# Layer-1 feed-forward on f16 halves, gate products joined to qkv, few-row products on 128 rows, unit addresses formed one triple ahead

## The chip, the core and the metric

The kernel runs on one core of a Trainium2 chip. The metric is the device time of one execution in microseconds (us). The core has five engines that run their own instruction queues in order and wait for each other on semaphores: TensorE (PE in the profile; PEld is its loading of the stationary operand), VectorE (DVE), ScalarE (ACT), GpSimd (POOL) and SyncE (SP).

## The reference, cut to what matters

The input is 32 sequences of 256 tokens, each token a vector of 128. Everything is a residual stream `x`, in f32:

```
x = x + 0.5 * L0_ffn(layernorm(x))      # 8 experts, top 2, and one shared
x = x + L0_attn(layernorm(x))           # linear attention, 32 heads, group norm
x = x + 0.5 * L0_ffn(layernorm(x))
x = x + 0.5 * L1_ffn(layernorm(x))      # 8 experts of 32 hidden values, top 1
x = x + L1_attn(layernorm(x))           # gated recurrence, 8 heads
x = x + 0.5 * L1_ffn(layernorm(x))

def L1_ffn(xt):
    top1 = argmax(xt @ Wg.T)
    xhat = layernorm(xt)
    for e in range(8):
        h = gelu((xhat * ln_scale[e] + ln_bias[e]) @ W1[e] + b1[e])
        y = y + (top1 == e) * (h @ W2[e] + b2[e])

# L1_attn: q, k, v = h @ Wq.T, h @ Wk.T, h @ Wv.T, and three gates
gate(W, b) = sigmoid(h @ W.T + b)        # W is 8 x 128, for beta, ig, og
```

## The kernel before

**Tiles and stages.** `x` stays on the chip. It is cut into 16 chunks of 512 tokens (T = 4 tiles of 128). Three stages overlap. The heads (three lanes) take a chunk through the norm, the gate, the shared expert and, between the two layer-0 feed-forwards, the attention. The units are the routed experts: tokens are scattered by expert to DRAM (`scatter`, an indirect DMA on POOL), fetched back in blocks of 128 and worked on in 76 units of four blocks; results are fetched with another indirect DMA (`fetches`). The last part of the span, from about 735 us, holds layer 1: the first feed-forward of a chunk (`ffn1` on the lanes mid), the attention's `front` and `back`, and the second feed-forward (`ffn1` on the lanes last). `ffn1` is called 32 times, `front` and `back` 16 times each.

**Order.** No engine chooses its order by itself. `turns` holds, for each engine, a string with one letter for each step (u and w are units, a to c heads, m n l o the feed-forwards of layer 1, t front, v back, r routing, s scatter, f fetch, p preparation, z a matmul whose result nobody reads). Each engine runs the steps in the order of its own string and waits, where it must, for a mark that another engine sets. PSUM has six banks that are handed out in turn; TensorE waits for the mark in `ring.free_at` before it writes a bank again.

**Layer-1 feed-forward on TensorE, `ffn1`.** Step 3 turns the normed chunk (4 transposes) and ACT copies it to `s.xt` in f32. Step 4 multiplies each tile by the gate, 4 f32 products of 8 columns (L740; the trace shows two records for each f32 product). DVE picks the best expert and builds a mask; step 6 turns it. Step 7 makes, for j = 0 and 1, one f32 product of 512 columns with the hidden weights of four experts (L757) and adds `sel1` times the mask (L759), which pushes all experts that were not chosen far below zero; the product with `sel1` contracts over 8 rows. ACT applies gelu. Step 8 multiplies by the second weights (L767, L771) and DVE adds the result to `x` (L1359).

**Layer-1 attention, `front`.** Step 0 turns the chunk. Step 1 first makes the gates, 4 f32 products of 24 columns into one bank (L791, read by DVE at L1387 to L1393), then q, k and v, 4 f32 products of 384 columns in a bank each (L797), which ACT copies out with the norm's factor (L1630, L1632). The gates' chain goes on from DVE's `zc` (L1393) to ACT's exponential (L1618).

**Biases.** Three outputs get a bias by a product that contracts over 3 rows, bf16 parts of the bias against ones: L544 (32 times), L613 (16) and L870 (16). An f32 product with full rows follows each.

**Units, `project`.** Each unit has two projections of two banks; for each bank and each of four blocks TensorE runs a triple: the high half of the weights against both halves of the rows, then the low half against the high half (L712). The place of the weights depends on the block's expert, held in a register; the two addresses of a triple, one in `w_hi` and one in `w_lo`, are computed by register instructions right in front of the matmul that uses them.

## Time and profile before

| | us |
|---|---|
| median of 3 runs | 1345.95 |
| lowest and highest run | 1339.19, 1349.72 |
| the profiled execution | 1347.7 |
| its span, first to last instruction | 1345.9 |

| engine | busy us | share of the span |
|---|---|---|
| PE | 1190.7 | 88% |
| DVE | 1059.0 | 79% |
| ACT | 807.7 | 60% |
| POOL | 676.6 | 50% |

The mean granted TensorE clock is 0.954 of full speed. Busy time is the union of an engine's records: matmuls are pipelined, so a matmul's own duration is longer than the distance from its start to the next one's. Where the cost of a matmul is wanted, the distance of the starts is read. The chain of waits is followed back from the last instruction, at each step to what released it.

### The profile page before, as it was taken

To read this page: it belongs to the slowest core of one execution; us is meant where nothing else is said; L and a number is where in the kernel's file an instruction comes from. 1 tells how busy PE (TensorE), PEld (TensorE's weight loads), DVE (VectorE), ACT (ScalarE), POOL (GpSimd) and SP (SyncE) were. 2 spreads that over 40 slices of the span, in tenths; PEclk is the share of its full clock that TensorE was granted. 3 is DMA by queue.
4 is the path that set the end of the run, shared out by engine and by line. 5 is a ranking of instruction groups with operands and counts; after the bars stand their busy time and mean duration, and the time that the engine had idled before them with its cause. 6 is when DMAs were issued, how large, how long until landed. Compare 5 with 4: busy or idle time off the path is not lost.

```text
span 1345.9 us, 39493 instructions
## 1 busy us (share of the span) xinstructions
PE 1190.7 (88%) x14344; PEld 918.0 (68%) x14344; DVE 1059.0 (79%) x3479; ACT 807.7 (60%) x1350; POOL 676.6 (50%) x727
## 2 busy tenths in 40 slices
PE   2866898898889979878998899999999999899997
PEld 1533776776677767656776678777777767676774
DVE  4888899988797989898878777767867689785652
ACT  1455677646645646555665777667746566556652
POOL 0157666777777777877777523415323634310100
PEclk9877999999999999999999999999979899899986
DMA  9001343533354332324343311222100111000001
GB/s 320 1 25 59 96 117 102 120 88 99 99 118 108 89 99 69 98 74 95 87 124 106 82 38 44 65 55 68 32 17 14 33 31 30 14 18 1 26 3 32
DMA packets 172958, 94.13 MB, mean 70 GB/s; under 512 B 98539, under 2 KB 163206, under 8 KB 172646
## 3 DMA queue, kind: packets, MB, share of 16 engines
q1 hardware_dynamic: 112838, 34.26, 10.5%
q0 software_dynamic: 16384, 33.59, 8.9%
q10 hardware_dynamic: 43552, 23.74, 6.4%
q8 instruction: 125, 2.05, 0.7%
q14 instruction: 59, 0.48, 0.1%
HBM read 25.98 MB, written 45.61 MB: 53 GB/s over the span
## 4 chain that ended last, share of the span: by engine, by line
PE 49%; DVE 30%; ACT 6%; issue 6%; POOL 5%; SPq 2%; DMA 2%; ACTq 0%; POOLq 0%; DVEq 0%
PE bank L712 10%; PE bank L757 4%; PE bank L771 3%; DVE heads_store L986 3%; DVE x L1018 2%; POOL rows L1725 2%; PE bank L728 2%; PE bank L928 2%; PE bank L797 2%; PE bank L740 2%; PE sums L945 2%; PE bank L559 2%; SPq L1791 1%; PE bank L759 1%; PE bank L841 1%
## 5 line engine op out<-in xcount | busy, mean ns | idle before, releaser
L1725 POOL DMA_INDIRECT rows<-store,r_slot x256 | 262.0, 1024 | 123.8 <-issue 73.3
L1742 POOL DMA_INDIRECT y_in<-ys,r_result x256 | 274.7, 1073 | 91.9 <-issue 71.2
L712 PE MATMUL bank<-u_xp,w_hi 128*128 128x128 f16 x2432 | 261.7, 222 | 10.7 <-DMA u_xp<-rows 3.8
L712 PE MATMUL bank<-u_xp,w_lo 128*128 128x128 f16 x1216 | 244.4, 221 | 0.0
L712 PEld LDWEIGHTS bank<-u_xp,w_hi 128*128 x2432 | 176.5, 99 | 35.2 <-issue 15.0
L712 PEld LDWEIGHTS bank<-u_xp,w_lo 128*128 x1216 | 120.0, 99 | 3.0
L1694 POOL TENSOR_SCALAR ve_last<-mv_last 128x4 f32<-128x4 f32 x16 | 3.3, 208 | 171.7 <-DVE mv_last L979 171.6
L559 PE MATMUL bank<-heads_store,w_hi 128*128 128x512 f16 x256 | 80.9, 399 | 5.7 <-DVE u_gated_odd L1330 3.1
L757 PE MATMUL bank<-heads_store,f_w1s 128*128 128x512 f32 x128 | 77.8, 692 | 0.7 <-ACT heads_store L1602 0.7
L1018 DVE SCALAR_TENSOR_TENSOR x<-y_in,r_weight,x 128x128 f32<-128x128 f32 x256 | 72.8, 346 | 1.6 <-DMA y_in<-ys,r_result 0.5
L771 PE MATMUL bank<-w_packed,heads_store 128*128 128x128 f32 x512 | 69.0, 291 | 0.0
L1495 ACT COPY heads_store<-bank 128x512 f32<-128x512 f32 x64 | 37.0, 584 | 52.3 <-PE bank L510 40.2
L771 PEld LDWEIGHTS bank<-w_packed,heads_store 128*128 128x128 f32 x512 | 64.6, 205 | 0.0
L1470 DVE TENSOR_TENSOR store<-store,bank 128x512 f32<-128x512 f32 x64 | 40.8, 680 | 25.9 <-ACT store L1671 15.9
L986 DVE TENSOR_SCALAR heads_store<-x,mv_head,rstd_head 128x128 f32<-128x128 f32 x192 | 55.3, 366 | 7.0 <-POOL rstd_head L1696 6.8
L1694 POOL TENSOR_SCALAR ve_front<-mv_front 128x4 f32<-128x4 f32 x16 | 3.2, 199 | 111.3 <-DVE mv_front L979 110.9
L1525 ACT ACTIVATE heads_store<-bank,sc 128x512 f32<-128x512 f32 x64 | 43.1, 681 | 21.3 <-PE bank L559 19.8
L1696 POOL TENSOR_TENSOR rstd_head<-ve_head,half_neg 128x4 f32<-128x4 f32 x48 | 53.3, 1111 | 4.0
L1606 ACT ACTIVATE heads_store<-bank,f_b1s 128x512 f32<-128x512 f32 x64 | 42.0, 686 | 20.3 <-PE bank L759 19.5
L559 PE MATMUL bank<-heads_store,w_lo 128*128 128x512 f16 x128 | 51.1, 399 | 0.0
L1498 ACT COPY heads_store<-bank 128x1024 f16<-128x1024 f16 x32 | 32.2, 1009 | 28.6 <-PE bank L518 27.8
L1064 DVE TENSOR_TENSOR heads_store<-bank,heads_store 128x512 f32<-128x512 f32 x64 | 43.1, 682 | 7.9 <-ACT heads_store L1525 7.4
(389 smaller groups left out, 3217.2 us busy)
## 6 DMA issues: line engine op xcount, KB each, us to landing
ys<-u_y_even ACTq DMA_DIRECT2D x38, 256.0 KB
ys<-u_y_odd ACTq DMA_DIRECT2D x38, 256.0 KB
u_xp<-rows SPq DMA_TRANSPOSE x304
x<-x_dram SPq DMA_DIRECT2D x16, 256.0 KB, 5.7
rows<-store,r_slot POOLq DMA_INDIRECT x256
y_in<-ys,r_result POOLq DMA_INDIRECT x256
out_dram<-x SPq DMA_DIRECT2D x16, 256.0 KB, 2.5
rows<-blank SPq DMA_DIRECT2D x48, 64.0 KB
```

The source lines that it names most:

```text
L559: ins = pe.matmul(B[:], wp[:, part, E, which, :], s.xp[:, xp, :], start=(n == 0), stop=(n == 2))
L712: ins = pe.matmul(B[:, of_block[j]], of_expert(wp, e, F16, part, which), xp_rows[:, xp, of_block[j]], start=(n == 0 and j == 0), stop=(n = ...
L757: pe.matmul(B[:], f1_w1s[:, j * P:(j + 1) * P], s.xt, start=True, stop=False, skip_group_check=True)
L771: ins = pe.matmul(Y[:, by_t[t]], s.gs[j][:, by_t[t]], const["f1_w2"][:, j, :], start=False, stop=(t == T - 1 and j == 1), skip_group_check ...
L986: ins = dve.tensor_scalar(out[:, t, :], xc(c)[:, t, :], s.mv[:, t, 0:1], s.rstd[:, t:t + 1], ALU.subtract, ALU.mult)
L1018: ins = dve.scalar_tensor_tensor(xt, y[:, t, i, :], w[:, i, t0 + t:t0 + t + 1], xt, ALU.mult, ALU.add)
L1064: s.by_vector.mark(dve.tensor_tensor(h, ring[s.name, "h", l, c, part, 1][:], h, ALU.mult), "h", l, c, part)
L1525: s.by_scalar.mark(act.activation(t, ring[s.name, "h", l, c, part, 0][:], ACT.Copy, scale=sc31[:]), "h", l, c, part)
L1606: mark(act.activation(s.gs[j], ring[s.name, "gelu", c, j][:], ACT.Gelu, bias=f1_b1s[:, j:j + 1]), "gelu", c, j)
L1696: s.by_pool.mark(pool.tensor_tensor(s.rstd[:], s.ve[:], half_neg[:], ALU.pow), "rstd", which, c)
L1725: pool.indirect_dma_start(row_dram[g], bass.IndirectOffsetOnAxis(route.slot[g][:, i, t:t + 1].bitcast(U32), 0), rows[:, groups[g].first * ...
L1742: pool.indirect_dma_start(fetch.y[i][:, t, k, :], None, y_dram[g], bass.IndirectOffsetOnAxis(route.result[g][:, k, t0 + t:t0 + t + 1].bitc ...
```

## The change

The layer-1 feed-forward keeps its turned input as two f16 halves in the same bytes: ACT copies the high half out of PSUM, and a new DVE step 3 subtracts it from the bank to give the low half. The gate and the hidden weights are scaled by powers of two, split into f16 halves in two new preparation steps, and each f32 product becomes three f16 products. The gelu gets a scale that undoes the factors. The bank of the transposes is free after DVE's subtraction.

The gates' 24 columns are put behind the 384 of q, k and v: one product of 408 columns for each tile. DVE reads the gates out of each tile's bank with one instruction for each tile instead of two for all, and ACT copies v after it.

`sel1`, `row_bias` and `ones_b` are used with all 128 rows, the unused rows of the first two being zero, so the mask and bias products contract over 128 rows.

`place_weights` lowers the two addresses of the next triple before the current triple's matmuls; the first triple's addresses are lowered with `load_experts`.

The indirect DMAs lose their bounds check. All the sequences in `turns` are new; the first steps of each stage stand at nearly the same place in them as before, and there are 12 letters z instead of 9.

```diff
-        f1_w1s = sb("f1_w1s", [P, E * 32])
+        f1_hi = sb("f1_hi", [P, E * 32], F16)
+        f1_lo = sb("f1_lo", [P, E * 32], F16)
+        g1_hi = sb("g1_hi", [P, E], F16)
+        g1_lo = sb("g1_lo", [P, E], F16)
...
+        a1_w = sb("a1_w", [P, 3 * D + 3 * NH1])
+        a1_wqkv, a1_wg = a1_w[:, 0:3 * D], a1_w[:, 3 * D:]
...
-        row_bias = sb("row_bias", [3, 3, D], BF16)
+        row_bias = sb("row_bias", [P, 3, D], BF16)
...
+            s.xp = s.xt.bitcast(F16).rearrange("p (k n) -> p k n", k=2)
...
-                    pe.matmul(Y[:], ones_b[0:3, :], row_bias[:, 0:1, :].broadcast_to([3, T, D]), start=True,
+                    pe.matmul(Y[:], ones_b[:], row_bias[:, 0:1, :].broadcast_to([P, T, D]), start=True,
...
                     if u < 2:
                         load_experts(pe, use)
+                        place_weights(pe, use, 0, 0, 0)
...
                     if u + 2 < groups[g].units:
                         load_experts(pe, (l, g, u + 2))
+                        place_weights(pe, (l, g, u + 2), 0, 0, 0)
...
+            def place_weights(pe, use, part, which, j):
+                if not isinstance(pe, Counted):
+                    last = (part * NE * 2 + which) * F * 2 + (F - 1) * 2
+                    for table in (w_hi_bytes, w_lo_bytes):
+                        pe.lower_ap(table[:, bass.ds(held[use][j] + last, 2)].bitcast(F16))
...
                         e = held[use][j]
+                        if j < PER_UNIT - 1:
+                            place_weights(pe, use, part, which, j + 1)
+                        elif (part, which) != (1, 1):
+                            place_weights(pe, use, part + which, 1 - which, 0)
...
                 if k == 3:
-                    transposed(s, "ffn1", c, s.by_scalar)
+                    transposed(s, "ffn1", c, s.by_vector, "lo")
                 elif k == 4:
-                    on.wait_ge(*s.by_scalar.at("xt", "ffn1", c))
+                    on.wait_ge(*s.by_vector.at("lo", "ffn1", c))
+                    on.wait_ge(*prep.by_vector.at("f1"))
                     M = bank(s.name, "logits1", c)
                     for t in range(T):
-                        ins = pe.matmul(M[:, t * E:(t + 1) * E], s.xt[:, by_t[t]], const["f1_gate"][:],
-                                        start=True, stop=True)
+                        for n, (xp, gp) in enumerate(((0, g1_hi), (1, g1_hi), (0, g1_lo))):
+                            ins = pe.matmul(M[:, t * E:(t + 1) * E], s.xp[:, xp, by_t[t]], gp[:], start=(n == 0),
+                                            stop=(n == 2))
...
-                        pe.matmul(B[:], f1_w1s[:, j * P:(j + 1) * P], s.xt, start=True, stop=False,
-                                  skip_group_check=True)
-                        s.by_tensor.mark(pe.matmul(B[:], sel1[:, j, :], s.maskt[0:E, :], start=False, stop=True,
+                        for n, (wp, xp) in enumerate(((f1_hi, 0), (f1_hi, 1), (f1_lo, 0))):
+                            pe.matmul(B[:], wp[:, j * P:(j + 1) * P], s.xp[:, xp, :], start=(n == 0), stop=False,
+                                      skip_group_check=True)
+                        s.by_tensor.mark(pe.matmul(B[:], sel1[:, j, :], s.maskt, start=False, stop=True,
...
-                    B = bank(s.name, "z", c)
                     on.wait_ge(*prep.by_vector.at("a1_centred"))
                     for t in range(T):
-                        ins = pe.matmul(B[:, t * G:(t + 1) * G], s.xt[:, by_t[t]], a1_wg[:], start=True,
-                                        stop=True)
-                    s.by_tensor.mark(ins, "z", c)
-                    ring.free_at((s.name, "z", c), s.by_vector, "z", c)
-                    for t in range(T):
                         B = bank(s.name, "qkv", c, t)
-                        s.by_tensor.mark(pe.matmul(B[:, 0:3 * D], s.xt[:, by_t[t]], a1_wqkv[:], start=True,
+                        s.by_tensor.mark(pe.matmul(B[:, 0:3 * D + 3 * NH1], s.xt[:, by_t[t]], a1_w[:], start=True,
...
+                elif k == 3:
+                    on.wait_ge(*s.by_scalar.at("xt", "ffn1", c))
+                    mark(dve.tensor_tensor(s.xp[:, 1, :], ring[s.name, "xn", "ffn1", c][:], s.xp[:, 0, :], ALU.subtract),
+                         "lo", "ffn1", c)
...
-                    on.wait_ge(*s.by_tensor.at("z", c))
                     on.wait_ge(*s.by_pool.at("rstd", "attn1", c))
-                    mark(dve.tensor_tensor(s.z, ring[s.name, "z", c][:, 0:T * G].rearrange(
-                        "p (t g) -> p t g", t=T), wide(s.rstd[:], G), ALU.mult), "z", c)
-                    on.wait_ge(*at("z", c))
-                    mark(dve.tensor_tensor(s.z, s.z, const["a1_bg"][:].unsqueeze(1).broadcast_to([P, T, G]),
-                                           ALU.add), "zb", c)
-                    on.wait_ge(*at("zb", c))
+                    for t in range(T):
+                        on.wait_ge(*s.by_tensor.at("qkv", c, t))
+                        mark(dve.scalar_tensor_tensor(s.z[:, t, :], ring[s.name, "qkv", c, t][:, 3 * D:3 * D + G],
+                                                      s.rstd[:, t:t + 1], const["a1_bg"][:], ALU.mult, ALU.add),
+                             "z", c, t)
+                    on.wait_ge(*at("z", c, T - 1))
                     mark(dve.tensor_scalar(s.zc, s.z, Z_LEAST, None, ALU.max), "zc", c)
...
                         on.wait_ge(*s.by_tensor.at("qkv", c, t))
+                        on.wait_ge(*s.by_vector.at("z", c, t))
...
-                        rows[:, groups[g].first * T + t, :, :].rearrange("p k d -> p (k d)"), None, bounds_check=spare - 1,
-                        oob_is_err=False).then_inc(scattered[g], 16)
+                        rows[:, groups[g].first * T + t, :, :].rearrange("p k d -> p (k d)"), None).then_inc(scattered[g], 16)
```

## Rows read from the trace of the kernel before

**Rows 1.** The page: shares of the span that the chain of waits spends on each engine.

```profile
PE 49%; DVE 30%; ACT 6%; issue 6%; POOL 5%; SPq 2%; DMA 2%; ACTq 0%; POOLq 0%; DVEq 0%
```

**Rows 2.** By stretch: us, busy PE, PEld, DVE, ACT, POOL, granted clock, DMA, GB/s.

```profile
0.00:145.00 145.00, 84.64 (x567) 51.75 (x567) 109.81 (x395) 64.56 (x90) 55.33 (x68) 0.87 0.32 100
145.00:735.00 590.00, 519.93 (x5319) 418.96 (x5319) 512.70 (x1704) 355.35 (x554) 438.88 (x457) 0.99 0.39 100
735.00:1346.00 611.00, 586.11 (x8463) 447.32 (x8461) 436.46 (x1382) 387.74 (x707) 182.38 (x204) 0.94 0.13 34
```

**Rows 3.** The chain of waits from 735 to 1346 us: shares by line.

```profile
by line: PE bank L757 9.7%; PE bank L771 7.7%; PE bank L712 4.5%; PE bank L928 4.5%; PE bank L797 4.2%; PE bank L740 3.9%; PE sums L945 3.7%; PE bank L759 3.0%; PE bank L841 2.9%; PE bank L884 2.4%; PE bank L915 2.2%; PE bank L874 2.1%; PE 
```

**Rows 4.** The chain of waits from 145 to 735 us: shares by line.

```profile
by line: PE bank L712 17.5%; issue 8.8%; DVE heads_store L986 3.6%; PE bank L728 3.2%; DVE x L1018 2.9%; POOL rows L1725 2.9%; PE bank L559 2.4%; DVE heads_store L1064 2.0%; DVE stats_head L975 2.0%; DVE u_linear_odd L1323 1.8%; DVE u_linea
```

**Rows 5.** Timeline of PE: start, length, instructions; one visit's hidden and mask products.

```profile
1036.50 1.02 PE L757 MATMUL bank<-heads_store,f_w1s 128*128 128x512 f32 x2
1037.45 0.39 PE L759 MATMUL bank<-heads_store,w_sel 8*128 8x512 bf16 x1
1037.77 1.13 PE L757 MATMUL bank<-heads_store,f_w1s 128*128 128x512 f32 x2
1038.83 0.39 PE L759 MATMUL bank<-heads_store,w_sel 8*128 8x512 bf16 x1
1039.05 0.38 PE L870 MATMUL bank<-row_bias,w_ones_b 3*128 3x512 bf16 x1
```

**Rows 6.** Timeline of PE: unit triples, then a head's f16 gate and shared expert.

```profile
501.33 0.28 PE L712 MATMUL bank<-u_xp,w_hi 128*128 128x128 f16 x2
...
501.50 0.28 PE L712 MATMUL bank<-u_xp,w_hi 128*128 128x128 f16 x2
...
502.55 0.27 PE L712 MATMUL bank<-u_xp,w_hi 128*128 128x128 f16 x2
...
502.77 0.27 PE L712 MATMUL bank<-u_xp,w_hi 128*128 128x128 f16 x2
...
503.01 0.19 PE L534 MATMUL bank<-g_hi,heads_store 128*128 128x8 f16 x2
...
503.31 0.59 PE L559 MATMUL bank<-heads_store,w_hi 128*128 128x512 f16 x2
...
503.96 0.59 PE L559 MATMUL bank<-heads_store,w_hi 128*128 128x512 f16 x2
```

**Rows 7.** Timeline of PE: layer-1 gate, attention gates, q k v, and what follows.

```profile
1022.98 0.96 PE L740 MATMUL bank<-w_packed,heads_store 128*128 128x8 f32 x8
1023.82 1.07 PE L791 MATMUL bank<-a_wg,heads_store 128*128 128x24 f32 x8
1024.73 2.83 PE L797 MATMUL bank<-a_wqkv,heads_store 128*128 128x384 f32 x8
1027.39 0.55 PE L859 MATMUL sums<-store 128*128 128x64 f32 x4
```

**Rows 8.** Timeline of PE: a bias product and the f32 products behind it.

```profile
537.17 0.38 PE L544 MATMUL bank<-row_bias,w_ones_b 3*128 3x512 bf16 x1
537.49 1.16 PE L548 MATMUL bank<-w_packed,heads_store 128*128 128x128 f32 x8
538.48 0.39 PE L725 MATMUL bank<-by_expert,r_member 128*128 128x128 bf16 x4
```

**Rows 9.** Line L712 alone: the register instructions; ns min/median/max, first and last start.

```profile
L712 PEldq ALU_OP  x2128: 32/32/42, 138.6 to 949.2; - x194
```

**Rows 10.** Single lines of DVE: ns min/median/max, first and last start us, form.

```profile
L1035 DVE SCALAR_TENSOR_TENSOR store<-heads_store,store x32: 656/684/746, 50.7 to 694.1; 128x512 f16<-128x512 f32 x32
...
L1387 DVE TENSOR_TENSOR heads_store<-bank,rstd_front x16: 248/257/258, 752.9 to 1277.2; 128x96 f32<-128x96 f32 x16
```

**Rows 11.** Waits: who waited for whom, us in total, times, longest us.

```profile
ACT heads_store L1618 <- DVE heads_store L1393: 28.8, 13, 7.0
```

**Rows 12.** The page's groups: busy us, mean ns of one, idle before and its cause.

```profile
L1725 POOL DMA_INDIRECT rows<-store,r_slot x256 | 262.0, 1024 | 123.8 <-issue 73.3
```

More of the change, by code:

```diff
@@ L45 @@
 SETUP_STEPS = 18
-PREP_STEPS = E + 5
+PREP_STEPS = E + 6
 WEIGHT_BYTES = 512
@@ L173, in build @@
             at += n
-        for name, shape in (("sel", [P, NH1, HALF]), ("nsel", [P, NH1, HALF]), ("sel1", dram["sel1"].shape),
+        for name, shape in (("sel", [P, NH1, HALF]), ("nsel", [P, NH1, HALF]), ("sel1", [P, 2, P]),
                             ("later", [P, HALF]), ("ident_b", [P, P]), ("tri_b", [P, P]), ("ones_b", [P, P])):
@@ L179, in build @@
         ident_h = sb("ident_h", [P, P], F16)
-        f1_w1s = sb("f1_w1s", [P, E * 32])
+        f1_hi = sb("f1_hi", [P, E * 32], F16)
+        f1_lo = sb("f1_lo", [P, E * 32], F16)
+        g1_hi = sb("g1_hi", [P, E], F16)
+        g1_lo = sb("g1_lo", [P, E], F16)
+        f_back, f_inv, f_scale = (sb("f_" + k, [P, NM]) for k in ("back", "inv", "scale"))
         f1_b1s = sb("f1_b1s", [P, 2])
@@ L504, in bank, with transposed @@
                 return b
-            def transposed(s, which, c, reader):
+            def transposed(s, which, c, reader, done="xt"):
                 M = bank(s.name, "xn", which, c)
@@ L511, in transposed @@
                 s.by_tensor.mark(ins, "xn", which, c)
-                ring.free_at((s.name, "xn", which, c), reader, "xt", which, c)
+                ring.free_at((s.name, "xn", which, c), reader, done, which, c)
             def split_turned(M, src, n=T):
@@ L634, in prepared @@
                     on.wait_ge(*prep.by_vector.at("a1"))
-                    pe.matmul(M[:, 64:64 + 3 * D], minus_mean[:], a1_wqkv[:], start=True, stop=True)
-                    prep.by_tensor.mark(pe.matmul(M[:, 64 + 3 * D:64 + 3 * D + 3 * NH1], minus_mean[:], a1_wg[:],
-                                                  start=True, stop=True), "a1")
+                    prep.by_tensor.mark(pe.matmul(M[:, 64:64 + 3 * D + 3 * NH1], minus_mean[:], a1_w[:], start=True,
+                                                  stop=True), "a1")
                     ring.free_at(("prep", "a1"), prep.by_vector, "a1_centred")
+                elif k == E + 4:
+                    on.wait_ge(*prep.by_vector.at("f_max"))
+                    M = bank("prep", "f_max")
+                    prep.by_tensor.mark(pe.transpose(M[0:NM, 0:P], w_max[:], ident[:]), "f_max")
+                    ring.free_at(("prep", "f_max"), prep.by_vector, "f_maxt")
+                elif k == E + 5:
+                    on.wait_ge(*prep.by_vector.at("f_diag"))
+                    M = bank("prep", "f_back")
+                    prep.by_tensor.mark(pe.matmul(M[:, 0:NM], w_diag[:], ident[0:NM, 0:NM], start=True, stop=True),
+                                        "f_back")
+                    ring.free_at(("prep", "f_back"), prep.by_vector, "f_back")
             def routed(l, r, k):
@@ L1106, in split_biases @@
                 on.wait_ge(*at("bias_f"))
-                rest, row = bias_f, row_bias[:].rearrange("p e d -> p (e d)")
+                rest, row = bias_f, row_bias[0:3].rearrange("p e d -> p (e d)")
                 for k in range(3):
@@ L1598, in ffn1 @@
                         after_heads(on)
-                    turned(s, "ffn1", c)
+                    on.wait_ge(*s.by_tensor.at("xn", "ffn1", c))
+                    mark(act.copy(s.xp[:, 0, :], ring[s.name, "xn", "ffn1", c][:]), "xt", "ffn1", c)
                 elif k == 6:
@@ L1606, in ffn1 @@
                         mark(act.activation(s.gs[j], ring[s.name, "gelu", c, j][:], ACT.Gelu,
-                                            bias=f1_b1s[:, j:j + 1]), "gelu", c, j)
+                                            bias=f1_b1s[:, j:j + 1], scale=f_back[:, 0:1]), "gelu", c, j)
             def attn1_front(c, k):
@@ L1743, in fetches @@
                     fetch.y[i][:, t, k, :], None, y_dram[g],
-                    bass.IndirectOffsetOnAxis(route.result[g][:, k, t0 + t:t0 + t + 1].bitcast(U32), 0),
-                    bounds_check=groups[g].units * N - 1, oob_is_err=False).then_inc(fetched[i], 16)
+                    bass.IndirectOffsetOnAxis(route.result[g][:, k, t0 + t:t0 + t + 1].bitcast(U32), 0)).then_inc(fetched[i], 16)
             visits = {"head": head, "ffn1": ffn1, "front": attn1_front, "scatter": scatter, "fetch": fetches}
```

195 lines of the change are left out of this document (112 added, 83 removed).

## The prediction

> **What bounds the kernel now.** I read the chain of waits by engine first, then busy time by stretch, then the chain of each stretch by line, then the timeline for the distance between starts. The chain spends 49% on PE and 30% on DVE [rows 1]: TensorE sets the pace, with DVE as the second. By stretch the two differ. From 735 us, layer 1, PE is busy 586.1 of 611 us and DVE 436.5, 71% [rows 2]. From 145 to 735 us PE is busy 519.9 of 590 and DVE 512.7, so both are near their limit, and before 145 us DVE is ahead of PE [rows 2]. A microsecond off PE is therefore worth most behind 735 us, and that is where the changed products lie: L757 has 9.7% of that stretch's chain, L759 3.0%, L740 3.9%, L797 4.2% [rows 3].
>
> **Term 1, hidden and mask products (L757, L759).** One visit's pair of groups takes 1036.50 to 1039.05, 2.55 us [rows 5]. The last mask product is followed there by another product of few rows; where full rows follow, the distance behind it is 0.32 as between 1037.45 and 1037.77, not 0.22, so a usual visit is 2.65. The same shape in f16 exists: three products of 512 columns take 503.31 to 503.96, 0.65 us [rows 6]. With the mask product at a third of that, 0.22, a group is 0.87 and a visit 1.73. It saves 0.92 x 32 = 29.4 us of PE. How much was on the path: 12.7% of 611 is 77.6 us of the 84.8 that 32 visits take, 0.92 [rows 3, 5]. **27 us.**
>
> **Term 2, the gate (L740).** Eight records take 0.84 to 0.90 us [rows 7]; the layer-0 gate has just the new form, twelve f16 products of 8 columns, in 503.01 to 503.31, 0.30 us [rows 6]. 0.57 x 32 = 18 us; on the path stood 3.9% of 611 = 23.8 of about 28, 0.85. **15 us.**
>
> **Term 3, gates as columns of qkv (L791, L797).** L791's 0.91 us falls away. L797 takes 2.66 us for 4 x 384 columns [rows 7]; 408 columns make it 2.66 x 408/384 = 2.83. Net 0.74 x 16 = 12 us, of which 0.75 on the path (between the shares of L740 and the whole chain's 49%, nearer the first): **9 us.**
>
> **Term 4, bias products on 128 rows.** L544 starts 0.32 before L548 although 512 columns need 0.217 (a third of 0.65), and L548's eight records take 0.99 instead of L740's 0.84 to 0.90 [rows 6 to 8]. The gap ahead shows at L759: two f32 passes need 2 x 2.66/8 x 512/384 = 0.89, and it starts 0.95 behind them [rows 5, 7]. So a product of few rows pays about 0.08 ahead, 0.10 itself and 0.06 behind, 0.24 us, 64 times: 15 us. 48 of the 64 lie before 735 us, where less of PE is path; I take 0.6. **9 us.** The bounds are 0 and 15.
>
> The Trainium skill ("TensorE: Matmul & The Clock Gate", LDWEIGHTS and the table of its last part) says that a load costs by its columns, not its rows, and that a 32-row product takes the time of a 128-row one; by that padding buys nothing and term 4 would be 0. No row shows full rows in these very products, so this stays open until the new trace.
>
> **Term 5, unit addresses.** Each of the 1216 triples of L712 needs two addresses; 2128 of these register instructions stand in one row [rows 9]. A triple takes 0.17 us at the start of a run of them (501.33 to 501.50) and 0.22 to 0.24 further on (502.55, 502.77, 503.01) [rows 6]: TensorE's queue runs dry there. L712 has 17.5% of 590 and 4.5% of 611 us of chain, 131 us [rows 3, 4]. If the early addresses hid the whole difference, a mean triple of about 0.22 would come down to 0.17: 30 us at most. But the number of register instructions is the same and the queue is in order, so where their own rate is the limit, moving them buys nothing: lower bound 0. What is surely gained is that a triple that waited for a bank or rows can start at once. Nearer the lower end: **8 us.**
>
> **Term 6, no bounds check.** Scatters spend 73.3 us of POOL's time on "issue" between them, 0.3 us each [rows 12]; on the path is 2.9% of 590, 17 us [rows 4]. A quarter less would be 4 at most; with 0 as the other end, **2 us.**
>
> Sum of the gains on the path: 27 + 15 + 9 + 9 + 8 + 2 = 70 us.
>
> **What comes back.** (a) DVE's new subtraction reads 128x512 and writes f16, like L1035's 684 ns [rows 10]: 32 x 0.68 = 22 us of DVE. The gates take four instructions instead of two of 257 ns [rows 10]; four cost at most 1.03 us, at least about what the two did, so 0 to 0.5 us more, I take 0.3 x 16 = 5. DVE behind 735 us goes from 436 us to about 463, and the stretch shrinks to some 560, so its share rises from 71% to 83%: the cover is thin. I put 0.6 of 27 on the path, 16 us; bounds 0.3 and 1. What queues behind the subtraction on DVE are the units' openings, the attention's masks and the adds to `x` that free banks. (b) The gates' chain starts later: the last column comes after four qkv products, 2.83 us, instead of after L791's 0.91. ACT already waits 28.8 us for that chain's DVE end, 13 of 16 times [rows 11]. 1.9 x 16 = 31 us of delay, most of it covered by other chunks' products; a sixth, 5 us. Bounds 0 and 15. (c) Two more preparation steps put some ten short DVE instructions into the first 145 us, where DVE is ahead (109.8 against 84.6 [rows 2]): 2 us. Together 23 us.
>
> The mask product's 128 rows, the gelu's scale and the larger clears at the start cost nothing: same columns, same instruction, and a DVE that waits for the loads then. ACT's copy keeps its place and length.
>
> **Result.** 70 - 23 = 47 us off the profiled execution's 1347.7 (its span 1345.9 and 1.8 around it) gives 1300.7. The median shown, 1345.95, lies 1.7 below that execution: **1299 us**. The sequences are new, and no row prices them; they place the stages' first steps as before, so I count them at 0 and widen the range by 5 us each way.
>
> **Rivals.**
> - *The addresses were the brake.* Term 5 is 30 instead of 8: 1277 us. For it, the slow triples end as soon as another line's products come. Against it, the count stays. 0.15.
> - *DVE takes over in layer 1.* Its 27 us count whole and a quarter of PE's gain there (about 55 us) isn't reached, because steps then wait for DVE: 11 + 14 = 25 us worse, 1324. For it, 83% and an in-order queue [rows 2]; against it, PE stays the longer of the two, about 530 of 560 us. 0.2.
> - *Padding buys nothing*, by the rule cited under term 4, as a mechanism: the gaps around few-row products belong to the change of type, not of rows. Then term 4 falls away and term 1 loses 64 x 0.1 to 0.2 us: 16 to 20 us worse, 1317. Against it, L725 (bf16, full rows) starts only 0.99 behind eight f32 records that follow L544, without a gap of its own [rows 8]. 0.07.
> - *Slower.* The subtraction sits in the one place where a bank, PE's transposes, ACT's copy and DVE's queue meet; if the sequences place it so that DVE stands waiting, all behind it stand too. It decides from 70/32 = 2.2 us of path for each visit on (its 0.68 included) that the change isn't faster, and at 2.6 it is slower by over 1%, about 1362 us. For it, logits now wait for two engines; against it, in layer 1 PE's own products follow each other on the chain and wait little. 0.05.
> - *The change doesn't do what it says*: the freed PE time turns into waits for marks that still come when they did, under 13 us faster in all: about 1338. 0.06.
> - The forecast has the rest, 0.47.
>
> **How the numbers follow.** The forecast's own range is 1283 to 1315, from term 5 at 0 to 20 and (a) and (b) at their near bounds. The range given reaches into the first two rivals: 1273 to 1328 leaves out the slower case, the no-gain case and the outer ends of the others, about 2 in 10. Faster or slower by over 1% (13 us) is what a measurement of this kernel can tell: faster 0.47 + 0.15 + 0.19 + 0.07, less a little, 0.88; within 1%, 0.07; slower, 0.05.
>
> **What would show it.** Right: starts of the three f16 hidden products 0.65 us apart in all, a visit near 1.73; the gates' twelve in 0.3; L544's follower at 0.22 instead of 0.32; L791 gone; PE busy behind the heads down by 60 us or so and DVE's share up there. Term 5: triples in the later half of a run at 0.17 (rival) or still 0.22 (forecast). Wrong: the chain of layer 1 with DVE above its present share and new waits of PE for the subtraction, of DVE for ACT's copy, or of ACT for the gates well above 28.8 us. A granted clock clearly under the 0.94 of rows 2 in layer 1, because a leaner PE stands still more often, would also eat into the gain: the records there stretch at the lower of the two levels.

## The result, and the profile after

The new kernel takes 1308.6 us (median of 4 runs, 1302.72 to 1312.86), the kernel before 1345.01 us (4 runs): a ratio of 0.973 [0.970, 0.976]. In a second series it is 1305.84 against 1345.57, 0.969 [0.964, 0.975]. The gain is thus 36 to 40 us where 47 were forecast; the profiled execution alone, 1302.72 us, came within about 2 us of the 1300.7 worked out for it. The total was right. Terms 1 and 2 brought much less than they were to, and the sequences, counted at nothing, decide more than any term.

Page of the new kernel: busy time by engine, then the shares of the chain of waits.

```profile
PE 1091.2 (84%) x14383; PEld 876.3 (67%) x14412; DVE 1079.4 (83%) x3558; ACT 815.0 (63%) x1354; POOL 661.8 (51%) x727
...
DVE 45%; PE 28%; ACT 15%; issue 6%; POOL 4%; DMA 1%; SPq 1%; ACTq 0%; POOLq 0%; DVEq 0%
```

PE lost 99.5 us of busy time (1190.7 before), DVE gained 20.4 (1059.0 before), and the span fell by 45.0. The chain has turned round: PE led it with 49% [rows 1], now DVE leads with 45% against 28%.

The stretches that answer to those of before [rows 2], with the same columns (the last is 45 us shorter):

```profile
0.00:145.00 145.00, 82.96 (x630) 52.90 (x631) 114.42 (x413) 67.32 (x94) 57.76 (x72) 0.89 0.34 103
145.00:735.00 590.00, 493.50 (x5413) 409.98 (x5414) 525.85 (x1767) 366.42 (x576) 445.19 (x470) 0.98 0.41 102
735.00:1301.00 566.00, 514.78 (x8346) 413.42 (x8370) 439.10 (x1380) 381.22 (x685) 158.85 (x187) 0.92 0.13 34
```

Fixed times cut the work at different places, so I cut at an event that both kernels have, the start of the last unit product. Windows of the kernel before:

```profile
0.00:949.40 949.40, 810.21 (x8758) 634.88 (x8759) 783.32 (x2579) 577.77 (x916) 577.08 (x609) 0.97 0.34 90
949.40:1346.00 396.60, 380.47 (x5590) 283.16 (x5587) 275.65 (x901) 229.89 (x436) 99.51 (x118) 0.92 0.08 21
```

Windows of the new kernel:

```profile
0.00:928.70 928.70, 756.04 (x8772) 614.45 (x8783) 786.17 (x2605) 577.51 (x913) 561.43 (x604) 0.95 0.36 92
928.70:1301.00 372.30, 335.20 (x5615) 261.84 (x5631) 293.19 (x954) 237.45 (x442) 100.37 (x123) 0.94 0.09 23
```

Up to that product 54.2 us of PE gave 20.7 us of time, 0.38 per us. Behind it 45.3 us of PE gave 24.3, 0.54, against 17.5 us more of DVE. What differs between the two parts is how near DVE stands: in the first it is busy 83% of the time before and 85% after, right behind PE; in the tail PE is still clearly the busier of the two, 335 of 372 us against 293. No run changes this alone, so that it explains 0.38 and 0.54 is argued, not shown.

The products themselves. Timeline of PE, new kernel (start, length, instructions): one visit's hidden and mask products, the gate with what follows, and a bias product.

```profile
334.07 0.22 PE L738 MATMUL bank<-u_xp,w_lo 128*128 128x128 f16 x1
334.13 0.38 PE L548 MATMUL bank<-row_bias,w_ones_b 128*128 128x512 bf16 x1
334.34 0.83 PE L552 MATMUL bank<-w_packed,heads_store 128*128 128x128 f32 x6
...
1002.08 0.19 PE L768 MATMUL bank<-g_hi,heads_store 128*128 128x8 f16 x2
...
1002.39 0.64 PE L514 MATMUL bank<-w_packed,heads_store 128*128 128x128 f32 x4
1002.92 3.01 PE L818 MATMUL bank<-a_w,heads_store 128*128 128x408 f32 x8
1005.76 0.39 PE L795 MATMUL bank<-by_expert,heads_store 128*128 128x128 bf16 x4
...
1017.69 0.59 PE L785 MATMUL bank<-heads_store,f_hi 128*128 128x512 f16 x2
1018.12 0.38 PE L785 MATMUL bank<-heads_store,f_lo 128*128 128x512 f16 x1
1018.34 0.38 PE L787 MATMUL bank<-heads_store,w_sel 128*128 128x512 bf16 x1
1018.55 0.59 PE L785 MATMUL bank<-heads_store,f_hi 128*128 128x512 f16 x2
...
1019.20 0.38 PE L787 MATMUL bank<-heads_store,w_sel 128*128 128x512 bf16 x1
1019.41 0.39 PE L776 MATMUL bank<-w_ident_b,heads_store 128*128 128x128 bf16 x4
```

A visit takes 1017.69 to 1019.41, 1.72 us (forecast 1.73); the gate 0.31 (0.3); the 408 columns 1002.92 to 1005.76, 2.84 (2.83). The bias product on 128 rows starts 0.06 behind its neighbour, as one unit product does behind another, and its follower 0.21 later, where 0.32 stood [rows 8]. Every duration taken from a row of the same form held, and not in this one place only: over the whole trace the median visit went from 2.66 to 1.74 us and the median gate from 0.90 to 0.37.

### The profile page after: what moved, and what is told of

The parts are those of the page before. It is cut to its first block, busy times and chain, and to the rows that moved or that the text cites. A ratio compares the mean times of both kernels' runs of the same rounds, so it can differ in the third digit from the quotient of the medians.

```text
span 1300.9 us, 37940 instructions
## 1 busy us (share of the span) xinstructions
PE 1091.2 (84%) x14383; PEld 876.3 (67%) x14412; DVE 1079.4 (83%) x3558; ACT 815.0 (63%) x1354; POOL 661.8 (51%) x727
## 4 chain that ended last, share of the span: by engine, by line
DVE 45%; PE 28%; ACT 15%; issue 6%; POOL 4%; DMA 1%; SPq 1%; ACTq 0%; POOLq 0%; DVEq 0%
PE bank L738 5%; DVE heads_store L1007 3%; DVE x L1039 3%; PE bank L799 2%; DVE stats_head L996 2%; DVE heads_store L1085 2%; PE bank L754 2%; POOL rows L1783 2%; PE bank L949 2%; PE sums L966 2%; PE bank L785 2%; DVE store L1526 1%; DVE x L1075 1%; DVE heads_store L1203 1%; PE bank L818 1%
## 5 line engine op out<-in xcount | busy, mean ns | idle before, releaser
L1783 POOL DMA_INDIRECT rows<-store,r_slot x256 | 260.6, 1018 | 111.1 <-issue 73.3
L1799 POOL DMA_INDIRECT y_in<-ys,r_result x256 | 262.2, 1024 | 76.9 <-issue 70.4
L738 PE MATMUL bank<-u_xp,w_hi 128*128 128x128 f16 x2432 | 227.6, 224 | 12.7 <-DMA u_xp<-rows 3.6
L738 PE MATMUL bank<-u_xp,w_lo 128*128 128x128 f16 x1216 | 219.4, 224 | 0.0
L738 PEld LDWEIGHTS bank<-u_xp,w_hi 128*128 x2432 | 194.1, 101 | 22.1 <-issue 16.7
L799 PE MATMUL bank<-w_packed,heads_store 128*128 128x128 f32 x512 | 65.8, 283 | 0.0
L799 PEld LDWEIGHTS bank<-w_packed,heads_store 128*128 128x128 f32 x512 | 61.4, 196 | 0.0
L1663 ACT ACTIVATE heads_store<-bank,f_b1s,f_back 128x512 f32<-128x512 f32 x64 | 46.9, 775 | 12.3 <-remote 10.3
L751 PE MATMUL bank<-by_expert,r_member 128*128 128x128 bf16 x304 | 30.7, 226 | 24.0 <-DVE u_linear_odd L1376 13.3
L949 PEld LDWEIGHTS bank<-store 32*64 32x64 f32 x2048 | 36.2, 143 | 20.5 <-issue 9.7
L1526 DVE TENSOR_TENSOR store<-store,bank 128x512 f32<-128x512 f32 x64 | 40.8, 679 | 10.4 <-ACT store L1729 9.0
L552 PE MATMUL bank<-w_packed,heads_store 128*128 128x128 f32 x256 | 37.6, 294 | 14.0 <-DVE heads_store L1071 13.8
L552 PEld LDWEIGHTS bank<-w_packed,heads_store 128*128 128x128 f32 x256 | 35.7, 206 | 19.1 <-DVE heads_store L1071 17.5
```

The costliest lines, as they stand in the source:

```text
L552: ins = pe.matmul(Y[:, by_t[t]], s.linear[:, by_t[t]], w2[:, E, :], start=False, stop=(t == T - 1), skip_group_check=True)
L738: ins = pe.matmul(B[:, of_block[j]], of_expert(wp, e, F16, part, which), xp_rows[:, xp, of_block[j]], start=(n == 0 and j == 0), stop=(n = ...
L799: ins = pe.matmul(Y[:, by_t[t]], s.gs[j][:, by_t[t]], const["f1_w2"][:, j, :], start=False, stop=(t == T - 1 and j == 1), skip_group_check ...
L949: ins = pe.matmul(B[i][halves[u], col:col + HALF], kt[strip[i], tokens], qpt[slot][strip[i], tokens], start=True, stop=True)
L1526: mark(dve.tensor_tensor(s.att[g], s.att[g], ring[s.name, "att", c, g][:], ALU.mult), "att", c, g)
L1663: mark(act.activation(s.gs[j], ring[s.name, "gelu", c, j][:], ACT.Gelu, bias=f1_b1s[:, j:j + 1], scale=f_back[:, 0:1]), "gelu", c, j)
```

## The experiments

Two groups of chips took part. On the first the kernel before takes 1345 us; on the second 1662 to 1682 us. The latter are told last, and nothing is compared across the groups but ratios.

**The new kernel once more.**

> The new kernel unchanged, on the chip of this call, as the reference for its own parts: the calls so far ran on two chips, one where the kernel before takes 1345 us and one where it takes 1682. On the first: ratio 0.973 as before. On the second the ratio isn't known; if VectorE sets the pace less there (TensorE's clock was 0.84 to 0.86 and its own issue time longer), the forecast's terms count more and the ratio is 0.96 to 0.97.

Measured: 1305.84 us, 0.969 [0.964, 0.975]. The gain is sound, and a little nearer to the forecast than in the first series.

**Layer 1's halves undone, all else new.** The feed-forward's gate and hidden products are f32 again, DVE's subtraction, the gelu's scale and the power-of-two factors are gone; the mask product keeps its 128 rows, and the preparation steps stay.

```diff
-for n, (wp, xp) in enumerate(((f1_hi, 0), (f1_hi, 1), (f1_lo, 0))):
-    pe.matmul(B[:], wp[:, j * P:(j + 1) * P], s.xp[:, xp, :], start=(n == 0), stop=False, ...)
+pe.matmul(B[:], const["f1_w1"][:, j * P:(j + 1) * P], s.xt, start=True, stop=False, ...)
```

> The new kernel with only the f16 halves of layer 1's feed-forward undone: f32 products of gate and hidden weights, no subtraction on VectorE. TensorE gets some 47 us more work, VectorE 22 us less. Theory 'TensorE still sets the pace in layer 1' (terms 1 and 2 less give-back a): 27 + 15 - 13, about 29 us slower than the new kernel's 1308.6, so 1333 to 1342. Theory 'VectorE has taken over': the added TensorE time is mostly covered and VectorE's 22 us come back, so 1300 to 1320.

Measured: 1312.92 us, 0.978 [0.973, 0.982]. Its windows, cut at its last unit product:

```profile
0.00:933.00 933.00, 764.15 (x8709) 616.76 (x8719) 781.55 (x2594) 576.98 (x914) 563.87 (x604) 0.95 0.35 92
933.00:1312.00 379.00, 352.07 (x5485) 275.39 (x5501) 282.75 (x931) 233.34 (x441) 100.35 (x123) 0.95 0.08 23
```

The halves are worth 4 to 7 us by the medians (1308.6 and 1305.84 against 1312.92) and 10.8 by the profiled spans; the intervals of this ratio and of the new kernel's first, 0.973 [0.970, 0.976], overlap, so the lower of these numbers is not clear of the noise. Over the whole span the halves take 25.0 us off PE's busy time (1116.2 to 1091.2). They also turn the chain round: without them it has PE at 40% and DVE at 36%, with them 28% and 45%. In the tail they take 16.9 us off PE (352.1 to 335.2), put 10.4 on DVE, and the tail is 6.7 us shorter.

**The same code in the sequences of before.** The last kernel again, with the turns of before; they hold one letter p more on TensorE, VectorE and ScalarE, and the last letters p of TensorE and VectorE stand at other places than before. All other letters are in the order of before.

```diff
-        turns = { ...the new sequences... }
+        turns = { ...those of before, with the added letters p... }
```

> The new kernel with two things undone: layer 1's feed-forward multiplies in f32 again (no second half, no subtraction on VectorE), and all engines follow the sequences of the kernel before (two letters p added). Left of the change: unit addresses, 128 rows, gates as columns, no bounds check. Theory 'parts carry the gain, the sequences nothing': the terms of the prediction left over, 9 + 9 + 8 + 2 less 5 for the late gates, about 20 us below 1345, so 1322 to 1328, and within 5 us of the same kernel in the new sequences. Theory 'the sequences carry it': 1340 or more here, and over 15 us slower than the same kernel in the new sequences.

Measured: 1359.79 us, 1.012 [1.008, 1.016]: slower than the kernel before. Between two kernels of the same computation and different order lie 47 us. (The instructions are the same but for three matmuls whose result nobody reads and four ACT table loads of 1.28 us, both more in the new, faster order.) Its windows:

```profile
0.00:953.00 953.00, 776.30 (x8711) 624.69 (x8721) 785.40 (x2604) 576.80 (x916) 562.57 (x609) 0.94 0.35 90
953.00:1359.00 406.00, 373.62 (x5484) 291.81 (x5498) 280.11 (x923) 229.16 (x435) 96.83 (x118) 0.89 0.08 20
```

The tail holds the same products (5484 records against 5485), yet they keep PE busy 373.6 us instead of 352.1, at a granted clock of 0.89 instead of 0.95. This is no accident of one execution: its four runs show 0.925 to 0.933 in all, those of the other order 0.944 to 0.949. Over the whole span PE is busy 1149.9 against 1116.2 us, so 34 of the 47 us stand there as PE time. One wait stands out too. Waits of ACT, this kernel:

```profile
ACT heads_store L1607 <- DVE heads_store L1382: 41.3, 15, 6.0
```

That is the gates' chain, 28.8 before [rows 11], 27.8 in the new kernel and 27.5 in the last one, the same code in the new order. Whether this wait makes PE stand still and the clock fall, or both follow from something else in the order, isn't separated.

**The new sequences on the code before.** The turns of the new kernel, without the letters of the added preparation steps, and nothing else of the change.

> The kernel before in every computation, with only the new sequences, once more. Theory 'the sequences carry the gain by themselves': 1310 to 1322 where the kernel before takes 1345. Theory 'sequence and code fit each other': 1345 to 1385 there, as the slower chip's ratio of 1.027 says (1381), so that neither the parts in the old sequences nor the new sequences with the old parts are faster.

Measured: 1352.43 us, 1.006 [1.003, 1.010], with 1192.5 us of PE as before. By themselves the new sequences lose 7 us, and the new code without the halves loses 15 in the old ones. Together they win 32. Neither is a saving that could be added to another. These ten runs show a clock of 0.937 to 0.952 (median 0.947), the kernel before beside them 0.948 to 0.965 (0.953).

**The early addresses alone, and all but them.** `place_weights` and its calls put into the kernel before; then taken out of the new one.

```diff
                         e = held[use][j]
+                        if j < PER_UNIT - 1:
+                            place_weights(pe, use, part, which, j + 1)
```

> The kernel before with only the unit addresses formed one triple ahead. The trace of the new kernel shows 1215 register instructions for them where 2432 were. Theory of the prediction (term 5, moved but not fewer, 8 us): 1337. Theory 'the two addresses of a triple now share one instruction, so TensorE's queue keeps up': the units' products lose about 33 us of distance between starts, and with 0.6 to 0.8 of it on the path the time is 1318 to 1326.

> The new kernel with the early addresses undone: each is formed in front of its matmul as before. If TensorE sets the pace among the units: 20 to 27 us slower than 1308.6, 1329 to 1336. If VectorE sets it there: the slower triples are covered, 1309 to 1318. The forecast's term (8 us) says 1317.

Measured: alone 1334.98 us, 0.993 [0.990, 0.997], some 10 us faster; without them the new kernel takes 1317.36, 0.980 [0.975, 0.984], 9 to 12 us slower than with them. Windows of the kernel before with the addresses early:

```profile
0.00:939.70 939.70, 780.02 (x8760) 616.55 (x8760) 780.77 (x2580) 576.40 (x916) 577.57 (x609) 0.95 0.35 91
939.70:1333.00 393.30, 376.62 (x5588) 280.47 (x5585) 275.62 (x900) 229.39 (x435) 99.44 (x119) 0.93 0.08 21
```

In the part with the unit products PE loses 30.2 us against before (780.0, not 810.2), and that part ends 9.7 us earlier: 0.32 us of time for each us of PE. The new kernel without them has 1129.4 us of PE, 38 more, for 9 to 12 us. Alone, in the old sequences, and as the last step, in the new ones, the early addresses bring about the same.

**The second group of chips.** The kernel before takes 1682.09 us in the first series there and 1662.34 in the second. On it: the new sequences alone (as above); the early addresses together with the 128 rows, in the old sequences; the new kernel with the gates' product and its bank apart again; and the new kernel with few rows, which ran in both series.

```diff
-pe.matmul(Y[:], ones_b[:], row_bias[:, 0:1, :].broadcast_to([P, T, D]), ...)
+pe.matmul(Y[:], ones_b[0:3, :], row_bias[0:3, 0:1, :].broadcast_to([3, T, D]), ...)
-s.by_tensor.mark(pe.matmul(B[:], sel1[:, j, :], s.maskt, ...))
+s.by_tensor.mark(pe.matmul(B[:], sel1[0:E, j, :], s.maskt[0:E, :], ...))
```

> The kernel before in every computation, with only the new sequences (without the letter p that the new preparation step needs). Theory 'most of the gain is the sequences', read from the f32 kernel that took 1312.9 in the new and 1359.8 in the old: 1310 to 1322, faster by 25 to 35 us with no instruction removed. Theory 'the new sequences fit only the new code': a wait that was placed for shorter products turns up, and it takes 1345 or more. The forecast counted the sequences at 0: 1345.

> The kernel before in its own sequences, with the unit addresses one triple ahead and the products of few rows on 128 rows; gates, f32 products and bounds checks as before. Addresses alone gave 1335. Theory 'few rows cost 0.24 us each, and the mask products 0.3': TensorE gets some 15 + 19 us shorter, and with a third of it on the path the time is 1320 to 1328. Theory 'padding buys nothing': 1333 to 1337. If this kernel is fast, what made the f32 kernel in the old sequences slow (1359.8) is the joined gates or the missing bounds check, the two things that it has and this one doesn't.

> The new kernel with the gates' products in a bank of their own again, ahead of q, k and v, and read by VectorE in two instructions. TensorE gets some 11 us more, VectorE a few less, and the gates' chain starts 1.9 us earlier in each of 16 chunks. Forecast (terms 3 and b): 9 - 5, so 4 us slower, 1310 to 1315. Theory 'the late gates cost more than the products': 1295 to 1305.

> The new kernel with mask and bias products on 8 and 3 rows again. The new trace shows 0.22 us from L548 to the product behind it where it was 0.32. Theory of the prediction: 128 products lose 0.2 to 0.24 us each, 25 to 30 us of TensorE, a third to a half of it on the path: 1317 to 1324. Theory 'padding buys nothing': 1309.

> The new kernel with mask and bias products on 8 and 3 rows again, once more. Each of the 128 products then costs TensorE 0.2 to 0.3 us more, 25 to 30 us. Theory 'a third on the path, as for the unit addresses (33 us of TensorE gave 10)': 8 to 12 us slower than the new kernel, ratio 0.976 to 0.981. Forecast (term 4 and the mask's part of term 1): 15 to 20 us, 0.981 to 0.985. 'Padding buys nothing': 0.969 to 0.973. On the slower chip, where the kernel before takes 1682, its ratio to that kernel was 0.994.

The last one puts one more instruction of 128x512 for each layer-1 chunk's result into DVE's queue of the new kernel:

```diff
+dve.tensor_tensor(s.xn.rearrange("p t d -> p (t d)"), ring[s.name, "ffn1", c][:], xf(c), ALU.add)
```

> The new kernel with one VectorE addition of 128x512 more in step 8 of each of the 32 layer-1 feed-forwards, written where nobody reads it: 32 x 0.68 = 22 us of VectorE work, as much as the new subtraction, with no new wait. Theory 'VectorE sets the pace in layer 1, and the subtraction ate the gain of the halves' (undoing them all cost only 4 us): 12 to 20 us slower than the new kernel's 1306, ratio 0.980 to 0.986 to the kernel before. Forecast (0.6 of it on the path): 13 us, 0.981. Theory 'VectorE is covered, the halves' gain was lost elsewhere': under 6 us, ratio 0.969 to 0.975.

The clock is the mean granted over the span of each run.

| kernel | us | ratio to before | clock |
|---|---|---|---|
| new sequences alone | 1732.67 | 1.027 [1.022, 1.033] | 0.84 |
| rows and addresses, old sequences | 1644.05 | 0.977 [0.969, 0.985] | 0.84 to 0.86 |
| gates apart | 1655.06 | 0.981 [0.976, 0.986] | 0.84 to 0.85 |
| few rows, first series | 1676.83 | 0.994 [0.990, 0.998] | 0.83 to 0.84 |
| few rows, second series | 1654.89 | 0.997 [0.993, 1.000] | 0.84 to 0.85 |
| more DVE work | 1657.59 | 0.996 [0.992, 0.999] | 0.83 to 0.85 |

Waits of PE, the new kernel with few rows, second series:

```profile
PE bank L738 <- issue: 86.3, 120, 2.3
```

its page, busy time and then the chain:

```profile
PE 1257.1 (76%) x14412; PEld 953.7 (58%) x14412; DVE 1086.4 (66%) x3558; ACT 818.3 (49%) x1354; POOL 652.5 (39%) x727
...
PE 44%; DVE 25%; issue 12%; ACT 10%; another core or an unknown queue 7%; DMA 1%; SPq 1%; POOL 0%; ACTq 0%; POOLq 0%; DVEq 0%
```

and the busy time of the new kernel with more DVE work:

```profile
PE 1237.4 (75%) x14412; PEld 966.0 (59%) x14412; DVE 1102.3 (67%) x3590; ACT 817.9 (50%) x1354; POOL 657.2 (40%) x727
```

PE stands for 86 us at the unit products and waits there for nothing that the profile shows. In all six kernels profiled on this group, 7 to 13% of the chain also goes to "another core or an unknown queue", which no chain of the first group has. So this group is slow for a reason of its own, which stays open, and its prices can't be carried over. The new kernel itself wasn't run on it, so the kernels derived from it can only be set against each other. Full rows with 16 us more of DVE (1102.3 against 1086.4) equal few rows without it, 0.996 and 0.997; full rows with the gates apart, 0.981, beat few rows with the gates joined, 0.994, in one series. Three readings hold without the new kernel. Few rows cost PE busy time, 1257.1 against 1237.4 us, 19.7. The new sequences alone lose here too, by more. And the early addresses with the 128 rows gain 2.3% in the old sequences (0.977 [0.969, 0.985]). By what was expected of that run, what made the f32 kernel slow in the old sequences is then the joined gates or the missing bounds check, the two things that it has and this one doesn't. That holds only as far as the two groups agree, and no run on the first one tests it; the wait for the gates' chain, 41.3 us there, speaks for the gates.

## Why the prediction was right, and where it was not

**Right: the durations.** Term 1's visit, term 2's gate, term 3's 408 columns and term 4's gaps all came out within 0.02 us, as shown above. For term 4 the Trainium skill ("TensorE: Matmul & The Clock Gate", the step on LDWEIGHTS) says that a load's time goes by its columns and that rows don't matter. The loads themselves agree: 91 ns at the median with 8 rows in the kernel before, 98 with 128 in the new one. What the rows change is when the load starts. Timeline of PEld at the mask product, the kernel before and then the new one:

```profile
1037.45 0.09 PEld L759 LDWEIGHTS bank<-heads_store,w_sel 8*128 8x128 bf16 x1 [0.76 <-issue]
1037.77 0.30 PEld L757 LDWEIGHTS bank<-heads_store,f_w1s 128*128 128x128 f32 x2 [0.23 <-issue]
```

```profile
1018.12 0.10 PEld L787 LDWEIGHTS bank<-heads_store,w_sel 128*128 128x128 bf16 x1
1018.34 0.31 PEld L785 LDWEIGHTS bank<-heads_store,f_hi 128*128 128x128 f16 x2
```

With 8 rows the load starts together with its product (1037.45 in [rows 5]), and the next load together with the next product; with 128 rows each starts 0.22 us ahead of its product, during the one before. So the prediction's gap is there on both sides of a few-row product, about 0.1 us each: behind it 0.32 against 0.21, ahead of the mask product, counted from the record before it, 0.53 against 0.43 (the latter with the halves undone and 128 rows). Few rows cost the 19.7 us of PE shown above, although the load itself takes no more time. The step from the page's sentence to "padding buys nothing" failed, and that rival falls as far as PE's own time goes. What the rows are worth in time, 9 us in the sum, stays open: nothing on the first group took them away alone. As a whole the part without the halves was well sized: terms 3 to 6 and the rows' share of term 1 (0.43 x 32 x 0.92 = 13), less the gates' part of (a), (b) and (c), make 31 us, and the kernel with f32 products is 32 us faster than before. But it has this in the new sequences only; of its parts, the early addresses alone keep their 10 us in the old ones.

**Right for the wrong reason: term 5.** 8 us forecast, 9 to 12 measured. Its premise was that the count of register instructions stays. It doesn't. New kernel, the line of the addresses (ns min/median/max, first and last start):

```profile
L714 PEldq FUSED_REGOPS  x1215: 37/37/79, 134.7 to 927.6; - x174
```

Timeline of PE, new kernel, the first, second, seventh and eighth triple of a run:

```profile
291.89 0.28 PE L738 MATMUL bank<-u_xp,w_hi 128*128 128x128 f16 x2
...
292.06 0.28 PE L738 MATMUL bank<-u_xp,w_hi 128*128 128x128 f16 x2
...
292.89 0.28 PE L738 MATMUL bank<-u_xp,w_hi 128*128 128x128 f16 x2
...
293.06 0.22 PE L738 MATMUL bank<-u_xp,w_hi 128*128 128x128 f16 x1
```

Standing next to each other, a triple's two address operations became one fused instruction: 1215 instead of 2432, of which 2128 stood in [rows 9] and 304 were fused already. A triple keeps to 0.17 us from the first to the eighth, where it had slowed to 0.22: over the whole trace the median of the fifth and later triples of a run was 0.22 before and is 0.17 now. That is the rival "the addresses were the brake", and PE's gain was its size, 34 us. Its 30 us of time did not come, only a third. The addresses were both moved and fused, and no run does one without the other, so which of the two speeds the triples is not shown.

**Wrong: the fractions on the path.** The forecast gave terms 0.6 to 0.92 of their PE time, from the lines' shares of the chain. Measured: 0.32 for the addresses, 0.38 for all up to the last unit product, 0.54 in the tail net of DVE's additions. The last can't be set beside the gross fractions: the forecast's own net for terms 1 to 3, (27 + 15 + 9 - 16 - 5) us of 59.4 of PE, is 0.5, close to it. It is among the units that the fractions fail: there 0.6 to 0.8 of 34 us would have been 20 to 27, and 9 to 12 came. Term 5 came near its time because its PE share was put far too low and the fraction that the other terms had wasn't used on it, which is luck. A share of the chain says who was waited for last, not how far behind the next one is. DVE was close behind. Waits of DVE from 735 us on, the kernel before:

```profile
DVE x L1359 <- PE bank L771: 31.1, 10, 13.8
DVE x L1474 <- PE bank L874: 28.1, 9, 8.6
...
DVE heads_store L1350 <- PE bank L740: 11.7, 9, 3.8
```

and the new kernel's:

```profile
DVE x L1416 <- PE bank L799: 17.6, 11, 7.4
...
DVE heads_store L1407 <- PE bank L768: 7.5, 6, 2.9
```

DVE's waits for PE's products shrink, and PE begins to wait for DVE. Waits of PE from 735 us on, new kernel:

```profile
PE bank L776 <- DVE heads_store L1024: 7.8, 4, 3.3
PE bank L514 <- DVE heads_store L1007: 7.3, 3, 4.3
PE bank L905 <- DVE store L1472: 5.1, 5, 2.4
...
PE bank L768 <- DVE heads_store L1403: 2.8, 5, 1.1
```

Between 735 and 1301 us of the kernel before, the largest such sum was 3.6 us. Terms 1 and 2 suffered most: beyond the rows' share they were to bring 0.49 x 32 x 0.92 + 15 = 29 us, less 13 for the subtraction, 16 in all; 4 to 7 came by the medians, 10.8 by the profiled spans, from 25.0 us of PE's busy time where 0.49 x 32 + 18 = 34 were counted. So of "DVE takes over in layer 1" the mechanism is there, chain and waits alike; its price was not, since PE stayed busy 90% of the tail.

**(a) DVE.** The subtraction is 682 ns as forecast. PE's gate waited for it only 2.8 us; DVE itself waits before it 7.2 us for ACT's copy, from 735 us on, a wait that the forecast named as a sign of trouble. Both are small beside its 21.7 us of work. Lines of DVE, new kernel:

```profile
L1403 DVE TENSOR_TENSOR heads_store<-bank,heads_store 128x512 f16<-128x512 f32 x32 | 21.7, 680 | 7.7 <-ACT heads_store L1656 7.7
L1445 DVE SCALAR_TENSOR_TENSOR heads_store<-bank,rstd_front,w_packed 128x24 f32<-128x24 f32 x64 | 12.1, 234 | 9.4 <-POOL rstd_front L1754 5.7 <-PE bank L818 3.6
```

With the gates at 12.1 instead of the 8.2 us of two lines before, the new work is 25.6 us, near the 27 of the forecast; DVE's busy time as a whole, in which overlapping records count once, rose by 20.4. Up to 735 us it stands at 640 (622 before), behind it at 439, not 463: layer 1's first mask product now starts at 718 us, not 742, so that part of layer 1 lies in the earlier stretch. The factor 0.6 has no measurement on the first group.

**(b) The gates' chain.** ACT's wait for it is 27.8 us in the new kernel, hardly less than the 28.8 of before. But the new sequences on the code before, with the gates still apart, have much less. Waits of ACT, that kernel:

```profile
ACT heads_store L1559 <- DVE heads_store L1334: 18.1, 10, 3.0
```

So with the gates joined this wait is 9.7 us longer in the new order (18.1 to 27.8) and 12.5 in the old one (28.8 to 41.3): of the two bounds, 0 and 15, the upper was the nearer, and not the 5 that the sum took. A wait of ACT is not yet time of the kernel, and other parts changed along with the gates; what the later start costs in time was not measured on the first group.

**A slip in the rival "slower".** 70/32 = 2.2 us for each visit leaves out the 7 us of (b) and (c); with them the limit is 63/32, 2.0 us. The result doesn't rest on it.

**Term 6** was at its lower end as far as the wait shows: scatters still wait 73.3 us for issue, the very number of [rows 12], though 512 short POOL instructions are gone. What did shrink is POOL's busy time, 661.8 us instead of 676.6; on the first group every kernel without the check has 659 to 664, every one with it 675 to 677. What that is worth in time wasn't measured. New kernel, the page's groups:

```profile
L1783 POOL DMA_INDIRECT rows<-store,r_slot x256 | 260.6, 1018 | 111.1 <-issue 73.3
```

**Counted at nothing, and wrong: the gelu's scale.** The same instruction of 128x512 in the new kernel, ns min/median/max:

```profile
L1663 ACT ACTIVATE heads_store<-bank,f_b1s,f_back x64: 767/777/782, 719.2 to 1293.7; 128x512 f32<-128x512 f32 x64
```

and with the halves undone:

```profile
L1654 ACT ACTIVATE heads_store<-bank,f_b1s x64: 679/687/697, 724.6 to 1304.3; 128x512 f32<-128x512 f32 x64
```

A scale read from a tile costs 90 ns, 64 times: 5.8 us of ACT. The Trainium skill states it ("ScalarE: Activation LUTs", What ACT_TABLE_LOAD costs): each pointer operand of one value per partition adds about 93 ns. I hadn't weighed it. What it cost in time isn't known; no run takes it away alone. The new sequences add about as much ACT work again, 124 table loads of 1.28 us where 120 were, 5.1 us.

**Counted at nothing, and wrong: the sequences.** "No row prices them" was true, and a range of 5 us each way wasn't: the same computation differs by 47 us between two orders. The sum came out because the order handed over with the code suited it, and nothing in the forecast had shown that it would: that part is luck.

**The clock.** The forecast named a lower granted clock as what would eat into the gain. The new kernel's eight runs show 0.933 to 0.951, the kernel before 0.948 to 0.965 in the second series. Within the kernel before, 1336.21 us goes with 0.965 and 1349.26 with 0.949, some 0.8 us for each 0.001. If that slope holds between kernels too, which no run shows, the gap of about 0.01 between the medians of the second series (0.942 and 0.953) is some 8 us, an estimate: about as much as the median fell short of the forecast there. In the profiled executions the lower clock is not where the forecast looked for it: up to the last unit product it fell from 0.97 to 0.95, behind it it rose from 0.92 to 0.94.

## What to carry to other kernels

Where a second engine is nearly as busy as the first, its share of the chain overprices a microsecond off the leader. Here PE was busy 85% and DVE 83% up to the last unit product, and a microsecond of PE was worth 0.32 to 0.38. So look at how long the second engine waits for the first, which is what can still shrink; how good a price that gives wasn't tried. A hand-written order is part of the code: measure a change with its order fitted, and measure the order alone before crediting either. Take durations from rows of the same form, and count an operand's kind (an address in a register, a scale in a tile) as part of the form.

## What the runs showed of the hardware that I had not expected

- Two address operations of TensorE's queue fuse when they stand next to each other (2432 to 1215 instructions). Fused and formed one triple ahead, they let the unit triples keep to 0.17 us where 0.22 was.
- A product of 3 or 8 rows costs about 0.1 us more than the same on 128 rows: its follower starts 0.32 behind it, not 0.21. Its load is as short (91 against 98 ns) but starts with its product and not ahead of it.
- An activation with a per-partition scale beside its bias takes 777 instead of 687 ns.
- Another order of the same computation came with another mean granted clock: 0.925 to 0.933 against 0.944 to 0.949, in every run.
- The time of one kernel follows the clock from run to run, 13 us between 0.965 and 0.949.
- One group of chips ran the kernel before in 1662 to 1682 us instead of 1345, at a clock of 0.84 to 0.87. The six kernels profiled there show 58 to 98 us of unexplained standstill at the unit products.
